# Two transformer layers on one core: weights cast in pieces of 512 columns, a context laid out by features, another order of the first loads

## The reference

```python
# layer 0, on x with context c
a  = layer_norm(x, g1, be1)
x  = x + softmax((a@Wq.T+bq)(a@Wk.T+bk).T / 4 + mask) (a@Wv.T+bv) @ Wo.T + bo
x  = x + (c @ Wg.T + bg)
x  = x + relu(layer_norm(x, g2, be2) @ W1.T + b1) @ W2.T + b2      # 1024 hidden
# layer 1, on x with the same context
x  = x + causal_attention(layer_norm(x, ln1)) @ sa_wo
y  = x + attention(q from layer_norm(x, ln2), k and v from c) @ ca_wo
y  = y + relu(layer_norm(y, ln3) @ mlp_w1 + mlp_b1) @ mlp_w2 + mlp_b2
```

## Time and profile before

| | us |
|---|---|
| median of 3 runs | 1629.85 (1628.0 to 1630.69) |
| profiled execution | 1625.86 |
| span of its trace | 1624.1 |
| PE / DVE / ACT / POOL busy | 1448.7 / 1193.5 / 1033.5 / 835.1 |
| mean granted clock of the tensor engine | 0.972 of full speed |

### The profile page before, as it was taken

How to read it: one execution, slowest core, us unless ns; L and a number is a source line. 1 busy time by engine, 2 the same in 40 slices (tenths; PEclk the granted TensorE clock), 3 DMA queues, 4 the chain that set the end, 5 groups by cost and what they waited for, 6 DMA issues and landing times.

```text
span 1624.1 us, 39350 instructions
## 1 busy us (share of the span) xinstructions
PE 1448.7 (89%) x13568; PEld 1184.2 (73%) x13568; DVE 1193.5 (73%) x3871; ACT 1033.5 (64%) x2089; POOL 835.1 (51%) x1125
## 2 busy tenths in 40 slices
PE   2799999999999999878887888888999999999986
PEld 2578888888888888765665656656777777777766
DVE  3788878888888887767777677787677776777642
ACT  3677777777777775555666656666666566665652
POOL 4455544545555565544434444545565555656533
PEclk8899999999999999989999999999999999999999
DMA  4554433443344443444454454554344433344200
GB/s 134 163 147 120 120 105 105 116 121 105 112 117 124 125 124 92 131 124 135 113 144 124 112 146 120 158 145 117 97 111 119 117 100 103 105 119 123 79 20 13
DMA packets 163605, 187.07 MB, mean 115 GB/s; under 512 B 15953, under 2 KB 140241, under 8 KB 163409
## 3 DMA queue, kind: packets, MB, share of 16 engines
q1 hardware_dynamic: 163408, 184.57, 40.1%
HBM read 125.78 MB, written 58.72 MB: 114 GB/s over the span
## 4 chain that ended last, share of the span: by engine, by line
PE 59%; ACT 15%; DVE 14%; issue 8%; POOL 2%; DMA 1%; SPq 1%; DVEq 0%; ACTq 0%; POOLq 0%
PE d_ps L451 23%; PE d_ps L713 8%; PE o_ps L587 8%; PE s_ps L509 6%; PE t_ps L523 6%; DVE prob L915 4%; ACT prob_t L761 4%; PE t_ps L557 3%; ACT q_stack L769 3%; PE m_ps L458 3%; ACT xt_hi L776 1%; ACT h_f L853 1%; DVE top L900 1%; DVE stats L921 1%; DVE q_part L1017 1%
## 5 line engine op out<-in xcount | busy, mean ns | idle before, releaser
L761 ACT ACTIVATE prob_t<-t_ps 128x384 f32<-128x384 f32 (+1 forms) x512 | 275.7, 550 | 354.8 <-PE t_ps L557 189.3
L509 PE MATMUL s_ps<-k_stack,q_stack 96*128 96x256 bf16 (+1 forms) x1536 | 288.9, 270 | 81.0 <-DVE top L915 50.1
L752 ACT ACTIVATE prob<-prob,neg_max 128x256 f32<-128x256 f32 x512 | 233.5, 509 | 115.3 <-DVE neg_max L915 113.1
L509 PEld LDWEIGHTS s_ps<-k_stack,q_stack 96*128 96x128 bf16 x1536 | 116.1, 99 | 175.9 <-issue 68.2
L557 PE MATMUL t_ps<-q_stack,k_stack 108*128 108x256 bf16 (+1 forms) x1024 | 205.5, 267 | 29.8 <-ACT prob_t L761 27.4
L1137 POOL TENSOR_TENSOR h_lo<-h_f,h_hi 128x512 fp32r<-128x512 f32 x128 | 164.9, 1288 | 119.8 <-DVE h_hi L1032 119.8
L915 DVE CUSTOM_DVE_ANT_0 prob<-s_ps,bias_sb 128x256 f32<-128x256 f32 x512 | 193.3, 418 | 30.3 <-PE s_ps L509 29.8
L900 DVE TENSOR_REDUCE top<-s_ps 128x2 f32<-128x512 f32 x256 | 172.6, 682 | 46.8 <-PE s_ps L509 43.3
L915 DVE CUSTOM_DVE_ANT_0 prob<-s_ps,causal 128x128 f32<-128x128 f32 (+1 forms) x512 | 157.4, 352 | 54.5 <-PE s_ps L509 52.9
L587 PE MATMUL o_ps<-prob_t,v_sb 128*17 128x256 f32 (+1 forms) x3072 | 195.4, 373 | 0.0
L451 PE MATMUL d_ps<-x2t_hi,w_hi 128*128 128x256 f32 x512 | 156.6, 306 | 15.3 <-ACT k_f L834 10.3
(11 more groups left out here) (127 smaller groups left out, 4051.2 us busy)
## 6 DMA issues: line engine op xcount, KB each, us to landing
parts<-q_part SPq DMA_DIRECT2D x96, 192.0 KB, 2.3
parts<-k_part SPq DMA_DIRECT2D x96, 192.0 KB, 2.3
q_stack<-parts SPq DMA_DIRECT2D x96, 192.0 KB, 3.3
k_stack<-parts SPq DMA_DIRECT2D x96, 192.0 KB, 3.3
q_stack<-parts SPq DMA_DIRECT2D x96, 128.0 KB, 3.1
k_stack<-parts SPq DMA_DIRECT2D x96, 128.0 KB, 3.2
ct_kept<-ct_hl SPq DMA_DIRECT2D x16, 512.0 KB, 3.5
x_in<-x_mid SPq DMA_DIRECT2D x32, 256.0 KB, 3.0
```

Source lines behind the costliest of these rows:

```text
L509: last = mm(s_ps[:, h % 2, q * S:q * S + n], q_stack[0:ROWS, t.par, head_of(t, h), q * P:(q + 1) * P], k_stack[0:ROWS, t.par, head_of(t, h ...
L752: last = nc.scalar.activation(prob[:, h % 4, q, :], prob[:, h % 4, q, :], ACT.Exp, bias=neg_max[:, h % 4, q:q + 1], scale=-1.0)
L761: nc.scalar.activation(prob_t[:, h % 8, 0:n], t_ps[:, h % 2, 0:n], ACT.Exp, scale=-1.0)\
```

## The change

The first three weights no longer go through the units: SP loads x of task 0, wq, ident, cols, wk, wv and rows in this order, each weight with a semaphore of its own; DVE casts them in slots 13 to 15 of step -2, POOL subtracts in slots 13 and 15. Engines wait for ident and cols only, and for rows where they are used. ACT's one-hot copies move, as a function with the same body, to step -1, slot 5, and POOL's sum of two rows to step -1, slot 10. The other nine units are cast and split in pieces of 512 columns, one a slot: o and the gate's in step -1, w1 in step 0 and w2 in step 1 (slots 8 to 11), q, k, v of passes 1 and 2 in three slots of steps 14 and 30, and w1 and w2 of the second layer one piece a step in slot 12 of steps 18 to 25. The host gives the context as features by tokens; the flip and ACT's copy are gone, and what waited for ACT's copy waits for the landing of the context or for the affine that last used the bank.

```diff
+START = (WQ, WK, WV)
-UNITS = (("a", 0, (WQ, WK, WV)), ("a", 0, (WO, WG)), ("w1", 0, ()), ("w2", 0, ()),
+UNITS = (("a", 0, (WO, WG)), ("w1", 0, ()), ("w2", 0, ()),
          ("a", 1, (WQ, WK, WV)), ("a", 1, (WO,)), ("w1", 1, ()), ("w2", 1, ()),
          ("a", 2, (WQ, WK, WV)), ("a", 2, (WO,)))
 LAG = 3
...
-UNIT_AT = {(-2, 14): (0,), (-1, 13): (1,), (0, 3): (2,), (0, 12): (3,),
-           (14, 12): (4,), (16, 13): (5,), (17, 9): (6,), (17, 14): (7,), (30, 12): (8,), (32, 13): (9,)}
-
-UNIT_LOAD_AT = {(-2, 2): 0, (-1, 0): 1, (-1, 14): 2, (0, 5): 3, (1, 0): 4, (15, 0): 5, (17, 1): 6, (17, 11): 7,
-                (18 - 1, 15): 8, (31, 0): 9}
-UNIT_QKV, UNIT_O = {0: 0, 1: 4, 2: 8}, {0: 1, 1: 5, 2: 9}
+PIECE_AT = {0: ((-1, 13), (-1, 14)), 1: ((0, 8), (0, 9), (0, 10), (0, 11)), 2: ((1, 8), (1, 9), (1, 10), (1, 11)),
+            3: ((14, 12), (14, 13), (14, 14)), 4: ((16, 13),), 5: ((18, 12), (19, 12), (20, 12), (21, 12)),
+            6: ((22, 12), (23, 12), (24, 12), (25, 12)), 7: ((30, 12), (30, 13), (30, 14)), 8: ((32, 13),)}
+UNIT_AT = {at: (u, n) for u, places in PIECE_AT.items() for n, at in enumerate(places)}
+UNIT_LOAD_AT = {(-1, 3): 0, (-1, 14): 1, (0, 12): 2, (1, 13): 3, (15, 0): 4, (17, 1): 5, (21, 13): 6, (26, 0): 7,
+                (31, 0): 8}
+UNIT_QKV, UNIT_O = {1: 3, 2: 7}, {0: 0, 1: 4, 2: 8}
 FIRST = (0,)
 GATE_AT, W2_AT = 10, (11, 12, 14)
 O_AT = (13, 14, 13)
-UNIT_W1, UNIT_W2 = {0: 2, 2: 6}, {0: 3, 2: 7}
+UNIT_W1, UNIT_W2 = {0: 1, 2: 5}, {0: 2, 2: 6}
...
-        c_in = sb("c_in", [P, TT, D])
+        c_in = sb("c_in", [P, KC, S])
...
+        start_landed = [sem(f"start_landed_{n}") for n in range(len(START))]
+        start_hi, start_lo = sem("start_hi"), sem("start_lo")
...
+        def piece_io(u, n):
+
+            _, place, hi, lo = unit_io(u)
+            flat = [t.rearrange("p r n -> p (r n)") for t in (place, hi, lo)]
+            return tuple(t[:, n * KC * D:(n + 1) * KC * D] for t in flat)
...
+            def start_weight(n):
+                sp.dma_start(stage[:, n * KC * D:(n + 1) * KC * D].rearrange("p (k n) -> p k n", k=KC),
+                             wa[0, START[n]].rearrange("(k p) n -> p k n", p=P)).then_inc(start_landed[n], 16)
+
+            sp.dma_start(x_in[:, 0], tokens(x[0])).then_inc(x_landed.of(Task(0, 0)), 16)
+            start_weight(0)
             sp.dma_start(ident_sb[:, :], ident).then_inc(const_landed, 16)
             sp.dma_start(cols_sb[:, :], cols).then_inc(const_landed, 16)
-            sp.dma_start(rows_sb[:, :, :], rows.partition_broadcast(P)).then_inc(const_landed, 16)
+            start_weight(1)
+            start_weight(2)
+            sp.dma_start(rows_sb[:, :, :], rows.partition_broadcast(P)).then_inc(rows_landed, 16)
...
-                        sp.wait_ge(unit_hi, u)
-                        sp.wait_ge(unit_lo, u)
+                        sp.wait_ge(unit_hi, sum(PIECES[:u]))
+                        sp.wait_ge(unit_lo, sum(PIECES[:u]))
+                    else:
+                        sp.wait_ge(start_hi, len(START))
+                        sp.wait_ge(start_lo, len(START))
...
-                if h == 1 and has(st.nxt2):
+                if h == 1 and has(st.nxt2) and st.s != -2:
...
-                        sp.wait_ge(ct_mm.sem, ct_mm.after(st.prev))
+                        sp.wait_ge(ct_l.sem, ct_l.after(st.prev))
                         sp.sem_inc(passed, 1)
-                    sp.dma_start(c_in[:, :, :], tokens(ctx[st.cur.b])).then_inc(ctx_landed.of(st.cur), 16)
+                    sp.dma_start(c_in[:, :, :], ctx[st.cur.b]).then_inc(ctx_landed.of(st.cur), 16)
...
-            pe.wait_ge(const_landed, 48)
+            pe.wait_ge(const_landed, 32)
...
-                    pe.wait_ge(ct_f.sem, ct_f.after(t))
+                    if st.old:
+                        pe.wait_ge(x2t_f.sem, x2t_f.after(st.old))
+                    else:
+                        pe.wait_ge(xt_f.sem, xt_f.after(st.nxt))
...
-                    weights(st.nxt, UNIT_QKV)
+                    if st.nxt.p:
+                        weights(st.nxt, UNIT_QKV)
+                    elif st.nxt.first:
+                        pe.wait_ge(start_lo, 1)
...
+                        pe.wait_ge(start_lo, 2)
...
+                        pe.wait_ge(start_lo, 3)
...
-                if h == 4 and has(st.prev, (0,)):
-                    pe.wait_ge(ctx_landed.of(st.prev), ctx_landed.after(st.prev))
-                    if st.old:
-                        pe.wait_ge(x2t_f.sem, x2t_f.after(st.old))
-                    else:
-                        pe.wait_ge(xt_f.sem, xt_f.after(st.nxt))
-                    flip(m_ps, c_in).then_inc(ct_mm.sem, 1)
...
-            for par in range(2):
-                heads = k_stack[ROWS:ROWS + TOP, par].rearrange("p (a j b) s -> p a j b s", a=2, b=2)
-                for b in range(2):
-                    for a in range(2):
-                        nc.scalar.activation(heads[:, a, :, b, :], one_hot[ROWS:ROWS + TOP, :].unsqueeze(2)
-                                             .to_broadcast([TOP, CH, S]), ACT.Copy, scale=-1.0).then_inc(chosen, 1)
+
+            def choose_rows():
...
-                if h == 5 and has(st.prev, (0,)):
-                    act.wait_ge(ct_mm.sem, ct_mm.after(st.prev))
-                    if st.old:
-                        act.wait_ge(x2t_h.sem, x2t_h.after(st.old))
-                        act.wait_ge(x2t_l.sem, x2t_l.after(st.old))
-                        act.wait_ge(ct_l.sem, ct_l.after(st.old))
-                    nc.scalar.activation(tf_b[:, :, :], m_ps[:, :].rearrange("p (k s) -> p k s", k=KC), ACT.Copy)\
-                        .then_inc(ct_f.sem, 1)
+                if h == 5 and st.s == -1:
+                    choose_rows()
...
-                    dve.wait_ge(ct_f.sem, ct_f.after(st.prev))
+                    dve.wait_ge(ctx_landed.of(st.prev), ctx_landed.after(st.prev))
...
-                    v.tensor_copy(ct_hi[:, :, :], tf_b[:, :, :]).then_inc(ct_h.sem, 1)
+                    v.tensor_copy(ct_hi[:, :, :], c_in[:, :, :]).then_inc(ct_h.sem, 1)
...
-                if st.s is not None:
-                    for u in UNIT_AT.get((st.s, h), ()):
+                if st.s == -2 and h >= 13:
+                    n = h - 13
+                    dve.wait_ge(start_landed[n], 16)
+                    v.tensor_copy(w_hi[:, START[n]].rearrange("p k n -> p (k n)"), stage[:, n * KC * D:(n + 1) * KC * D])\
+                        .then_inc(start_hi, 1)
+                if (st.s, h) in UNIT_AT:
+                    u, n = UNIT_AT[st.s, h]
+                    if n == 0:
                         dve.wait_ge(unit_landed, 16 * (u + 1))
                         unit_users_done(dve, u)
-                        _, place, hi, _ = unit_io(u)
-                        v.tensor_copy(hi, place).then_inc(unit_hi, 1)
+                    place, hi, _ = piece_io(u, n)
+                    v.tensor_copy(hi, place).then_inc(unit_hi, 1)
...
-            pool.wait_ge(const_landed, 48)
-            g.tensor_tensor(rows_sb[:, R_BO, :], rows_sb[:, R_BO, :], rows_sb[:, R_BG, :], ALU.add)\
-                .then_inc(causal_made, 1)
-            pool.wait_ge(causal_made, 6)
...
-                    sub(ct_lo[:, :, :], tf_b[:, :, :], ct_hi[:, :, :], ct_l.sem)
+                    sub(ct_lo[:, :, :], c_in[:, :, :], ct_hi[:, :, :], ct_l.sem)
...
-                if st.s is not None:
-                    for u in UNIT_AT.get((st.s, h), ()):
-                        pool.wait_ge(unit_hi, u + 1)
-                        _, place, hi, lo = unit_io(u)
-                        sub(lo, place, hi, unit_lo)
+                for n in {13: (0,), 15: (1, 2)}.get(h, ()) if st.s == -2 else ():
+                    pool.wait_ge(start_hi, n + 1)
+                    sub(w_lo[:, START[n]].rearrange("p k n -> p (k n)"), stage[:, n * KC * D:(n + 1) * KC * D],
+                        w_hi[:, START[n]].rearrange("p k n -> p (k n)"), start_lo)
+                if (st.s, h) in UNIT_AT:
+                    u, n = UNIT_AT[st.s, h]
+                    pool.wait_ge(unit_hi, sum(PIECES[:u]) + n + 1)
+                    place, hi, lo = piece_io(u, n)
+                    sub(lo, place, hi, unit_lo)
...
-    arrays = {"x": a["x"], "ctx": a["ctx_1024"], "mask": a["mask_BxSxS2_fk0"], "wa": wa, "wm1": wm1, "wm2": wm2,
+    arrays = {"x": a["x"], "ctx": a["ctx_1024"].reshape(B, S, KC, P).transpose(0, 3, 2, 1), "mask": a["mask_BxSxS2_fk0"], "wa": wa, "wm1": wm1, "wm2": wm2,
...
```

More of the change, by code:

```diff
@@ L495, in weights @@
                 if task.first:
-                    pe.wait_ge(unit_hi, units[task.p] + 1)
-                    pe.wait_ge(unit_lo, units[task.p] + 1)
+                    pieces = sum(PIECES[:units[task.p] + 1])
+                    pe.wait_ge(unit_hi, pieces)
+                    pe.wait_ge(unit_lo, pieces)
             def scores(st, h):
@@ L638, in slot @@
                         pe.wait_ge(y_done.sem, y_done.after(st.older))
```

(19 more changed lines are left out.)

27 lines of the change are left out of this document (17 added, 10 removed).

## The result

| | before | after |
|---|---|---|
| median, four runs each (us) | 1630.27 (1628.0 to 1632.95) | 1604.7 (1602.9 to 1605.87) |
| profiled execution (us) | 1625.86 | 1604.72 |
| span of its trace (us) | 1624.1 | 1602.9 |
| PE / DVE / ACT / POOL busy (us) | 1448.7 / 1193.5 / 1033.5 / 835.1 | 1440.9 / 1195.4 / 1024.7 / 837.6 |
| mean granted clock | 0.972 | 0.975 |

The ratio is 0.9842, 95% interval [0.9824, 0.9859]: 25.6 us less by the medians. The traces differ by only 21.2 us, because the profiled execution of before was faster than all four timed ones. Beside the experiments, before has medians of 1628.7 to 1628.9 us and single executions from 1625.54 to 1631.74, so part of the 25.6 lies in which executions of before were timed. What follows accounts for the 21.2; the other 4.4 belong to no step of these traces.

A forecast was written before the change was run, and what follows sets the result against it. Tensor engine bounds pass 0; elsewhere weight casts, holds and a falling clock cost time, and no engine is full in pass 1. 4.5 + 4.7 + 6.6 + 11 - 1.5 = 25.3 off 1629.85 gives 1604.5; 8-in-10 range 1595 to 1616.

The forecast's parts named there:

- Start: Before step 0: one-hot copies leave ACT's path and x loads first; first q product at 14.7, 4.5 us earlier.
- Steps 0 and 1: Whole weight casts and subtractions removed save 8.9 us, eight pieces in slots 8 to 11 cost 4.2: net 4.7.
- Pass 0: Steps 2 to 16: the flip leaves the tensor engine's path, 0.44 us in each of 15 steps, 6.6 us.
- Steps 17 and 18: Whole w1 and w2 work leaves these steps; they fall to 34.5 and 24.8 us, 11 us gained.
- Eight pieces: Steps 18 to 25, end of slot 12: each weight piece costs 0.2 us, 1.5 us in all.
- Rival 1: Pieces in passes 0 and 1 paid in full, 13.6 instead of 1.5 in steps 18 to 25; 1616.6; chance 0.13.
- rival 5: Slower: pass-1 pieces cost 3.1 us each, 25 in all, early pieces all held, 13.6; 1637; chance 0.03.
- Rival 2: Pass 0: the flip was no bound, DVE's end-of-step chain sets 37 us; gain 18.7, 1611; chance 0.13.
- Rival 3: Steps 17 and 18 give only 6, the mixed step needing its time for row maxima; 1609.5; chance 0.08.
- Rival 4: More than forecast: start 6.5, steps 0 and 1 at 8, steps 17 and 18 at 14; about 1596.5; chance 0.12.
- The rule on the shared port: DVE and POOL lock their port pair per instruction; cutting only spreads holds: 16 pieces 20 us, four subtractions 18.
- The table load: At the start, behind ACT's wait for the flip: 1.28 us by the trace; the skill page says about 2.7.

The follow-up runs named there:

- experiment 1: Changed kernel with only ACT's eight one-hot copies put back ahead of its first slot: 1608.55 us, ratio 0.9878.
- Experiment 5: Changed kernel with first-layer w2's four pieces moved to step 1 slot 13 and step 2 slots 0 to 2, next load later: 1601.28 us.
- experiment 12: Changed kernel with w1 and w2 pieces of the first layer later, later q, k, v whole, table load early, w1 loaded behind the mask: 1593.3 us.
- experiment 2: Kernel before the change with only the context laid out by features, without flip and ACT copy: 1623.63 us, ratio 0.997.
- kernel 4: Changed kernel with second-layer w1 and w2 still in four pieces each, but back in steps 17 and 18: 1616.81 us, ratio 0.9932.
- kernel 10: Changed kernel with the first of ACT's eight one-hot copies back ahead of its first slot, for an early table load: 1601.24 us, ratio 0.9832.
- kernel 3: Changed kernel with second-layer w1 and w2 cast and subtracted whole, in slot 12 of steps 18 and 22: 1608.66 us, ratio 0.9871.
- experiment 6: Changed kernel with q, k, v weights of passes 1 and 2 whole in slot 12 of steps 14 and 30: 1603.81 us, ratio 0.9842.
- kernel 7: Changed kernel with second-layer w1 in four pieces in slots 9 to 12 of step 17, w2 left at its new place: 1609.25 us.
- kernel 8: Changed kernel with second-layer w1 whole in slot 9 of step 17, w2 left in pieces at its new place: 1613.78 us, ratio 0.9906.
- kernel 9: Changed kernel with the load of w1 moved behind the mask and x of the next task, to step 0 slot 3: 1603.71 us, ratio 0.9851.
- kernel 11: Changed kernel with first-layer w2 pieces later, q, k, v of passes 1 and 2 whole, table load early, w1 loaded behind the mask: 1595.97 us.

## Why the prediction was right, and by what

The forecast of 1604.5 against 1604.7 measured is closer than its parts, and that closeness is luck. By the traces the gain is 21.2 and not 25.3; the forecast for the profiled execution, 1600.6, was 4.1 too low. Its terms, each against the trace:

- **Start, 4.5.** Step 0 starts 4.15 earlier and the first product 4.66 earlier; 14.7 was forecast for it, 14.51 came. The table load went behind the flip as forecast, and experiment 1 gives the term back when only the copies are moved. Right, within the 1 us by which step 0's start varies.
- **Steps 0 and 1, 4.7 net.** Measured 5.53 - 3.84 = 1.7. This is the term that was mis-sized. The removed part came out much as written: no cast over 1.8 beside a piece, the wait of 2.26 for the mask is gone, that of step 0 stays. (Of its 8.9 the prediction does not work out the first 4.3: the rows give 3.03 for the held k_part and 1.22 for the cast of w1.) The pieces cost more than the 4.2 forecast. I took "near the free end because a slot lasts longer than a piece holds"; but the piece's hold is not the matter alone. In slots 8 to 12 of a step DVE has stats, ve and the normalise of the next task in its stream, in a step in which DVE is nearly full, and ve, a cast and the normalise were each held by more than before (by 1.02, 0.73 and 0.92 in step 1). Experiment 5 moves w2's pieces and gets 4.2 back in step 1; experiment 12 moves w1's too and gets 2.5 in step 0. That is 6.7 instead of 4.2; with the 1.7 it puts what was removed at 8.4, an estimate from these steps.
- **Step 2**, for which the sum had the 0.44 of pass 0, loses 1.0 instead. Its clock was 0.97. Kernels 1, 2, 4, 5, 10 and 12 have it at 36.5, kernels 3, 6, 7, 8, 9 and 11 at 37.9 to 38.0, whatever their edit (below): it is not the change's.
- **Pass 0, 15 x 0.44 = 6.6.** Steps 3 to 13 give 4.7 (step 3 begins 4.83 earlier than before and step 14 9.49 earlier), step 4 with only 0.09 of it. Steps 15 and 16 give nothing, shown by experiment 2, and step 14 loses 0.42, of which experiment 6 shows that the three pieces cost 0.85. The forecast had seen step 14 at 37.09 with the whole cast and took from it that "the old and the new form both cost about nothing": that held for the old form only. The three pieces lie in the last slots of the step, where the chain runs over DVE; that this is the reason fits, but was not tested piece by piece. The mechanism (tensor engine as the bound) holds; by experiment 2 the number of steps in which it holds is 13 (2 to 14) and not 15.
- **Steps 17 and 18, 11.** Measured 15.3, beyond the end of 14. I set step 17 to its tensor time plus 2 us of waits, 34.5. It took 31.47 with the tensor engine busy for 31.15: no waits, and the half clock gone with them. The tensor time of the earlier trace rows, 34.28, already held the slow stretches; I took off too little for them. For w1, experiments 7 and 8 show that in step 17 more of it is the place than the size (5.0 and 1.7); for w2 the split is not shown.
- **Eight pieces, -1.5.** In steps 19 to 25, which have seven of them, the changed kernel takes 175.8 us (698.68 to 874.43), kernel 9 174.4 and kernel 1 176.1; without any piece there the kernel before takes 174.2, kernel 4 175.2 and kernel 2 175.8. So their price is under what these steps vary by. Rival 1 (13.6) and rival 5 (25) fall with it. The term is right in that it is small; 1.5 can't be confirmed.

The account closes: 4.15 + 1.7 - 1.0 + 4.3 (steps 3 to 16) + 15.3 - 1.5 (steps 19 to 25) - 1.7 (behind them, where nothing was changed but the pieces of step 30) = 21.2. The forecast was too high by 0.4, 3.0, 1.0, 2.3 and 1.7 and too low by 4.3, together 4.1 of the 25.3; that it meets the median all the same is the 4.4 by which the medians differ more than the traces. Two errors near 4 us, one in the terms and one in which executions of before were taken, cancel.

Rival 2 (the flip was no bound) falls with the 36.54 of step 7; for steps 15 and 16 it was right. Rival 3 falls with step 17. Rival 4 named 14 for steps 17 and 18 and was nearer there, and wrong for steps 0 and 1. Two slips in the prediction: rival 1 names the pieces of passes 0 and 1, but its 1616.6 counts those of pass 1 alone, and the chances of the forecast and the rivals make 1.00 without the 0.02 for no change.

**The rule on the shared port.** ve ends within 0.02 us of the subtraction that started 0.11 before it. In kernels 7 and 8 the two instructions of o_n end 0.62 and 0.61 us behind the end of the subtraction (666.01 and 669.78), wherever that is, which is a little less than the 0.76 they take alone. The Trainium skill, "SBUF — State Buffer", section "Who interferes with whom", has whoever issues first hold the pair for a whole instruction, with issue order and not the operation's shape deciding who blocks. The trace agrees: two columns waited for 512. What the forecast drew from it (the sum of the holds stays, only its spread changes) is true and did not decide; whether a held instruction stood on the path did.

**The table load.** It took 1.28 us in each trace shown, and in the changed kernel the affine began 0.01 us behind it; taking it off the path won 1.36. The Trainium skill, "ScalarE: Activation LUTs", section "What ACT_TABLE_LOAD costs", adds a drain of about 1.38 us to a load of about 1.28. So the prediction set the sum of both against the load: the load's duration agrees with the trace. No run here shows the drain on this first load.

## What to carry to other kernels

When a long operation on a shared resource has to be put somewhere, choose the place first and the size second: in a step whose bound is another engine (busy for 36.33 of 36.55 us) even pieces that fill DVE to 93% were free, in a step where the engine itself is nearly full four small ones cost 4 us, and in step 17 moving won 5.0 us and cutting 1.7. Size still counts: at the new places of steps 18 and 22, pieces were some 2 us a unit cheaper than the whole. Where the whole operation is already under cover, more and smaller ones can cost (0.85 us in step 14). And a busy engine that is "the bound" is so per place: after 0.44 us went, another engine was late in two of the steps, so a gain per step is to be counted over the steps whose chain stays on that engine.
